# One transfer of score maxima moved to ScalarE's queue, two image transfers merged, and the residual's second LayerNorm one pipeline step later

## The reference, cut to what matters

```
h = edge(x)                      # x: 32 images, 3 x 256 x 256; gray image, two 3x3 Scharr filters, (|gx|+|gy|)/2
h = concat([cls_tok, h])         # 257 tokens of 256 values per image
h = h + attention(layernorm(h))  # 16 heads of 16 values, causal; qkv with bias, output projection with bias
h = h + ffn(layernorm(h))        # gate, up, down with 704 hidden values; weights and activations rounded to 8 bits
```

## Time and profile before

| | |
|---|---|
| median of 3 runs | 1163.3 us (1157.46 to 1168.16) |
| the profiled execution, its own time | 1157.32 us |
| its span, first to last instruction | 1155.6 us |
| mean granted TensorE clock | 0.955 of full speed |
| busy: PE, DVE, ACT, POOL | 989.1, 814.8, 686.6, 538.1 us |
| DMA | 152.93 MB, mean 132 GB/s |

### The profile page before, as it was taken

The page is one execution under the profiler, slowest core; times in us unless marked ns, Lnnn a source line. Parts: engine busy times, 40 slices in busy tenths (PEclk is TensorE's granted clock), DMA queues, the critical chain, the costliest instruction groups (busy, mean ns, idle before and its releaser), DMA issues. The chain is left out here.

```text
span 1155.6 us, 28368 instructions
## 1 busy us (share of the span) xinstructions
PE 989.1 (86%) x9742; PEld 709.7 (61%) x9742; DVE 814.8 (71%) x1969; ACT 686.6 (59%) x1171; POOL 538.1 (47%) x685
## 2 busy tenths in 40 slices
PE   6768989899999999899999998999888888887665
PEld 5446766666667676667676676676676643333454
DVE  4565566766677777766777777666666449998787
ACT  1345555666666566666666666665553237876776
POOL 5335455565555655565556555655443242220000
PEclk7888999999999999999999999999998989998989
DMA  7665555555556555555565555453422005501874
GB/s 200 149 138 145 132 136 143 133 128 134 133 154 151 137 148 148 129 130 138 152 152 135 149 148 130 130 139 100 116 63 63 12 1 200 200 1 50 265 227 151
DMA packets 156017, 152.93 MB, mean 132 GB/s; under 512 B 28175, under 2 KB 152372, under 8 KB 153908
## 3 DMA queue, kind: packets, MB, share of 16 engines
q1 hardware_dynamic: 154440, 152.14, 48.7%
q10 hardware_dynamic: 1516, 0.01, 0.1%
HBM read 67.49 MB, written 28.35 MB: 83 GB/s over the span
## 5 line engine op out<-in xcount | busy, mean ns | idle before, releaser
L580 ACT ACTIVATE prob<-ST 128x772 f32<-128x772 f32 x256 | 209.5, 818 | 152.4 <-PE ST L1022 147.7
L788 DVE TENSOR_REDUCE mneg<-SX 128x2 f32<-128x258 f32 x256 | 107.5, 420 | 224.7 <-PE SX L1008 224.5
L1005 PE MATMUL SX<-kst,qst 96*128 96x257 bf16 (+1 forms) x1024 | 160.4, 250 | 18.3 <-DMA qst<-qpart 7.6
L790 DVE TENSOR_REDUCE mneg<-SX 128x2 f32<-128x514 f32 x256 | 173.9, 679 | 0.0
L1022 PE MATMUL ST<-qst,kst 98*128 98x256 bf16 (+2 forms) x1536 | 138.0, 222 | 16.3 <-DMA qst<-mpart 15.9
L465 POOL TENSOR_SCALAR_AFFINE_SELECT prob<-prob 128x1016 f32<-128x1016 f32 x128 | 142.6, 1114 | 0.0
L1008 PE MATMUL SX<-mask_s,ident_b 128*128 128x256 bf16 x512 | 142.4, 278 | 0.0
L1022 PEld LDWEIGHTS ST<-qst,kst 98*128 98x128 bf16 x1536 | 120.3, 99 | 34.5 <-DMA qst<-mpart 14.7
L1005 PEld LDWEIGHTS SX<-kst,qst 96*128 96x128 bf16 x1024 | 91.9, 99 | 64.3 <-issue 28.4
L1041 PE MATMUL G<-prob,vaug 128*32 128x256 f32 (+2 forms) x3072 | 116.2, 280 | 11.9 <-POOL prob L465 10.6
L1041 PEld LDWEIGHTS G<-prob,vaug 128*32 128x32 f32 x3072 | 82.7, 111 | 44.6 <-POOL prob L465 16.0
(11 more groups left out here) (232 smaller groups left out, 2056.9 us busy)
## 6 DMA issues: line engine op xcount, KB each, us to landing
kst<-kpart SPq DMA_DIRECT2D x192, 128.5 KB, 2.5
xin<-in_x SPq DMA_DIRECT2D x96, 256.0 KB, 4.1
gst<-gray_dram SPq DMA_DIRECT2D x96, 256.0 KB
qst<-qpart SPq DMA_DIRECT2D x192, 128.0 KB, 2.4
h_dram<-hb SPq DMA_DIRECT2D x8, 1280.0 KB, 4.6
gray_dram<-gray SPq DMA_DIRECT2D x64, 128.0 KB, 3.0
result<-oy SPq DMA_DIRECT2D x32, 256.0 KB, 3.6
hb<-h_dram SPq DMA_DIRECT2D x5, 1280.0 KB, 6.6
```

Source lines behind the costliest of these rows:

```text
L580: nc.scalar.activation(prob[:, g % 2, 2 * (u % 2):2 * (u % 2) + 2, 0:QEND], ST[:, :, 0:QEND], ACT.Exp).then_inc(exp_done, 1)
L788: nc.vector.tensor_reduce(mneg[:, 0, u // 4, 0, at], SX[:, :, S0:S0 + P + 1], AX.X, ALU.max, negate=True)
L790: nc.vector.tensor_reduce(mneg[:, 1, u // 4, 0, at], SX[:, :, S1:S1 + T], AX.X, ALU.max, negate=True).then_inc(max_done, 1)
L1005: mm(SX[:, r, at:at + k], qst[par][0:SR, 2 * u + r, P * t:P * t + P], kst[par][0:SR, 2 * u + r, 0:k], start=t == 1, stop=False)
```

## The change

It has three parts. (1) `max_rows(half 1)` is no longer issued by SP at the start of the next step, but by ACT at the end of its step, where ACT now waits for `msplit` (the DVE copy L805 at the start of the next step). (2) The three colour planes of an image are loaded by one DMA in place of three, and the gray image is saved by one in place of two. (3) `resid_stats`, the power on POOL and `x2` with its maxima are done for `bR = n-7` in place of `bO = n-6`, at other places of the step; `LAST` is 7, and `load_down` stands in step 33 in place of the end of step 32.

```diff
-        LAST = 6
+        LAST = 7
...
-        NW0, NW2 = 3, B + LAST - 2
+        NW0, NW2 = 3, B + 4
...
             def load_x(b, par):
-                for c in range(CH):
-                    sp.dma_start(xin[par][:, c, :, :], src[:, c]).then_inc(x_loaded[par], 16)
+                sp.dma_start(xin[par][:, :, :, :].rearrange("p c t w -> p (c t) w"), src).then_inc(x_loaded[par], 16)
...
             def load_down():
-                sp.wait_ge(gray_step, 2 * (B - 1))
+                sp.wait_ge(gray_step, 2 * B)
...
             # SP, step
-                max_rows(bT, odd, 1)
                 if valid(bO):
                     wait(sp, den_moved, bO, 64, 64)
...
                     sp.dma_start(rec[:, :], den[:, :]).then_inc(rec_moved, 16)
+                if isinstance(n, int) and n == B + 1:
+                    load_down()
                 if valid(bW):
...
-                    for t in range(QT):
-                        sp.dma_start(gray_dram[odd][1 + P * t:1 + P * t + P, 1:1 + IMG],
-                                     gray[:, t, :]).then_inc(gray_saved, 16)
+                    sp.dma_start(gray_dram[odd][1:1 + IMG, 1:1 + IMG].rearrange("(t p) w -> p t w", p=P),
+                                 gray[:, :, :]).then_inc(gray_saved, 16)
...
-                if isinstance(n, int) and n == B:
-                    load_down()
...
             # POOL, step
                 select(bT, 1)
+                if valid(bR):
+                    wait(pool, ln2, bR, LN, LN)
+                    wait(pool, x2_step, bR - 1, XS, XS)
+                    nc.gpsimd.tensor_tensor(rstd2[:, rows2(bR)], ve2[:, :], half[:, :], ALU.pow
+                                            ).then_inc(rs2_done, 1)
...
                 select(bS, 0)
-                if valid(bO):
-                    (the same for bO)
                 if valid(n):
                     wait(pool, gray_scaled, n, 3, 3)
...
             # ACT, end of the step
                 exponential(bS, 2)
                 if valid(n):
-                    wait2(act, x_loaded, n, par, 48)
+                    wait2(act, x_loaded, n, par, 16)
                     for c in range(CH):
                         nc.scalar.mul(xin[par][:, c, :, :], xin[par][:, c, :, :], GRAY[c]).then_inc(gray_scaled, 1)
+                if valid(bS):
+                    wait(act, msplit, bS, 2, 2)
+                    act.dma_start(qst[par][SR:SR + 2, 8:16, :], mpart[1][:, :]).then_inc(m_loaded[1], 16)
...
             # DVE, step
                 maxima(bS, 0)
                 (reciprocal of den for bO)
+                resid_stats(bR)
                 maxima(bS, 1)
+                if valid(bR):
+                    (x2, colmax, mean2 for bR)
                 maxima(bS, 2)
...
                 maxima(bS, 6)
-                resid_stats(bO)
                 (vlast and vaug for bP)
                 maxima(bS, 7)
-                if valid(bO):
-                    (x2, colmax, mean2 for bO)
...
-                if isinstance(n, int) and n == B + LAST - 1:
+                if isinstance(n, int) and n == B + 5:
```

More of the change, by code:

```diff
@@ L298, in _ @@
         def _(sp):
-            xv = x.rearrange("b c (t p) w -> b p c t w", p=P)
+            xv = x.rearrange("b c (t p) w -> b p (c t) w", p=P)
             def load_x(b, par):
-                src = xv[b] if isinstance(b, int) else xv[bass.ds(b, 1)].rearrange("o p c t w -> (o p) c t w")
-                for c in range(CH):
-                    sp.dma_start(xin[par][:, c, :, :], src[:, c]).then_inc(x_loaded[par], 16)
+                src = xv[b] if isinstance(b, int) else xv[bass.ds(b, 1)].rearrange("o p k w -> (o p) k w")
+                sp.dma_start(xin[par][:, :, :, :].rearrange("p c t w -> p (c t) w"), src).then_inc(x_loaded[par], 16)
             load_x(0, 0)
@@ L384, in step @@
                 if valid(bW):
-                    wait(sp, gray_saved, bW, 32, 32)
+                    wait(sp, gray_saved, bW, 16, 16)
                     wait(sp, conv_done, bC, 2, 2)
@@ L468, in step @@
             def step(n, par):
-                bC, bP, bS, bT, bO = n - 2, n - 3, n - 4, n - 5, n - 6
+                bC, bP, bS, bT, bR = n - 2, n - 3, n - 4, n - 5, n - 7
                 select(bT, 1)
+                if valid(bR):
[3 more added lines that the diff above has]
+                                            ).then_inc(rs2_done, 1)
                 if valid(bS):
@@ L503, in step @@
                 select(bS, 0)
-                if valid(bO):
[L505 to L508, removed]
                 if valid(n):
                     wait(pool, gray_scaled, n, 3, 3)
-                    wait(pool, gray_saved, n - 1, 32, 32)
+                    wait(pool, gray_saved, n - 1, 16, 16)
                     src = lambda c: xin[par][:, c, :, :]
@@ L854, in step @@
             def step(n, par):
-                bC, bP, bS, bT, bO = n - 2, n - 3, n - 4, n - 5, n - 6
+                bC, bP, bS, bT, bO, bR = n - 2, n - 3, n - 4, n - 5, n - 6, n - 7
                 odd = 1 - par
@@ L862, in step @@
                     nc.vector.reciprocal(den[:, :], den[:, :]).then_inc(rec_done, 1)
+                resid_stats(bR)
                 maxima(bS, 1)
+                if valid(bR):
+                    wait(dve, rs2_done, bR, 1, 1)
+                    for t in range(QT):
+                        nc.vector.tensor_scalar(x2[:, t, :], h2[:, row_of(bR, t), :].rearrange("p o d -> p (o d)"),
+                                                ag2[:, t, 0:1], rstd2[:, row_of(bR, t)],
+                                                ALU.subtract, ALU.mult).then_inc(x2_step, 1)
+                    wait(dve, x2_step, bR, XS, 2)
+                    nc.vector.tensor_reduce(colmax[:, rows2(bR)], x2[:, :, :], AX.X, ALU.max,
+                                            apply_absolute_value=True)
+                    nc.vector.tensor_reduce(mean2[:, rows2(bR)], ag2[:, :, 0:1], AX.X, ALU.max).then_inc(x2_step, 2)
                 maxima(bS, 2)
```

## The result

| | before | after |
|---|---|---|
| median | 1160.0 us (1155.0 to 1168.2, 13 runs) | 1148.5 us (1143.3 to 1154.6, 13 runs) |
| ratio of times, 95% interval | | 0.9895 [0.9867, 0.9922] |
| the profiled execution, its span | 1157.3, 1155.6 us | 1149.6, 1147.9 us |
| mean granted TensorE clock | 0.955 | 0.954 |

The change takes off 11.5 us by the medians and 7.7 us between the two profiled executions. The forecast was 1157, or 6.2 us less than the 1163.3 known then. The interval, 0.8 to 1.3% faster, has the 1% bound inside it.

The account below looks back on a forecast made before the run. The prediction took the steady step as bound by the chain PE -> ACT -> POOL -> PE. Start -0.5, loop -1, step 33 -0.7 and end -4.0 gave -6.2 us, from 1163.3 to 1157; range 1141 to 1167.

Parts of the forecast that it names:

- the removed holes: PE's idle gaps of 0.64 and 0.56 us before outputs(1), claimed to cost nothing in the steady step.
- select wait of some 0.8 us per step: Sign of a right forecast: PE's wait for POOL's select grows to this as other waits shrink.
- the gate: PE's wait at outputs(1) for POOL's select(1), taken to set the steady step's length.
- the 0.06 us margin: At outputs(1): PE arrives when POOL is ready, to 0.06 us, taken as showing the holes upstream cost nothing.
- Loop, -1 (0 to -3): Loop steps where PE comes late to the gate: moved residual statistics save 0 to 3 us, taken as 1.
- Step 33, -0.7: Step 33: load_down no longer holds up half 1, removing a 0.68 us wait of scores_t(4).
- Tail, -4.0 (-2.6 to -4.4): End of the block: earlier last reciprocal and rec issue save 2.6 us, with half 1's earlier arrival 4.0 in all.
- Start, -0.5: Launch start: merged transfers shorten SP's row of first issues, between 0 and -1.0 us.
- (a) The port on the gate: Loop: L852 before select(1) makes POOL wait, 0.36 us in each of 31 steps; +6 us, 1169; chance 0.11.
- (b) The holes count: Loop: the closed holes shorten each of 31 steps, -16 to -23 us; 1135 to 1142; chance 0.14.
- (c) Nothing arrives: Tail's PE work holds spread_rec and the loop gains nothing: 1163 us; chance 0.15.

Follow-up runs that it names:

- e7: The changed kernel plus three idle DVE reductions in front of split: 1146.45 us, ratio 0.9904 to the kernel before.
- e11: The changed kernel plus one small idle power on POOL behind the gray additions: 1178.1 us, ratio 1.0174 to the kernel before.
- e5: The kernel before with POOL's gray additions moved behind select(1) from step 8 on: 1159.2 us, ratio 1.0013.
- e3: The kernel before with part 3 of the change alone: 1150.35 us, ratio 0.9925.
- e10: The kernel before with part 3 for all but the last two images, load_down in step 33, LAST 6: 1155.8 us, ratio 0.9974.
- e2: The kernel before with part 2 of the change alone, the merged image transfers: 1160.5 us, ratio 1.0005.
- e4: The kernel before with only load_down moved one step later, to step 33 behind the rec transfer: 1154.8 us, ratio 0.9980.
- e8: The kernel before with part 3 for the last two images only: 1152.1 us, ratio 0.9933.
- e1: The kernel before with part 1 alone, half 1 of the maxima issued by ACT: 1158.5 us, ratio 1.0012.
- e9: The changed kernel with POOL's gray additions after select(1) and after the rstd2 power: 1162.7 us, ratio 1.0036 to the kernel before.
- e12: e9 with x2 and its reductions moved behind maxima(6), except in the last steps: 1163.6 us, ratio 1.0028 to the kernel before.

## Why the prediction was right, and where it was off

**The mechanism held, the size was low.** The forecast had PE bound by PE -> ACT -> POOL -> PE, and the removed holes worth little. The wait moved to `outputs(1)` (0 to 0.42 us a step), the chain kept its length (7.02 and 7.00), 0.6 us of delay in front costs nothing (e7), and 0.93 or 1.32 us more on the chain cost 0.95 or 1.32 a step (e11). Two qualifications. I expected a select wait of some 0.8 us per step; by the same count it is 14.9/24, about 0.62. And the gate was not the only bound before: opening it alone (e5) gives nothing that the medians show, so PE's own path through the holes was nearly as late, as the 0.06 us margin said, but I read that margin as one-sided.

**Loop, -1 (0 to -3).** Right in kind, undersized. Per step 459.7/18 = 25.54 us in place of 462.4/18 = 25.69, by the means of the groups: -2.7 us in 18 steps. Between the two marks the steps before lie between 25.56 and 25.86, and after between 25.43 and 25.55 but for one of 25.75. That the holes counted in those steps in which PE came late to the gate is my reading; no run shows it by itself. The early steps give no clear answer: up to the first mark the kernels of the table without the deferral need 303.9 to 311.1 us and those with it 303.3 to 311.1, counted by transposes. In this pair the changed kernel is 2.3 us later there, most of it from the copy at 204.50 / 202.45 to that at 257.05 / 260.42: 57.97 us after and 52.55 before, with e3 at 55.78, e10 at 52.33, e2 at 55.07. These overlap, and their cause stays open.

**Step 33, -0.7.** This step of the prediction failed, although it moved the forecast little. I put the long steps down to `load_down` in front of half 1. e4 takes that 0.68 us wait away and the steps stay long (82.86). What was long in them were stretches at 1.2 GHz; with the changed kernel they are gone, and that gives 2.8 us in this pair. The forecast priced TensorE at one clock.

**Tail, -4.0 (-2.6 to -4.4).** Right in mechanism, and in size for what it priced: `rec` is issued 3.82 us earlier, counted from the last transpose. Its -2.6 for the statistics alone is what e8 shows (2.6). The other 1.4 were put down to half 1 on ACT's queue and the earlier copy; part 1 is not needed for it, as e3, without part 1, issues `rec` 19.72 us after the transpose and the changed kernel 20.39. The clock, which was in no term, adds 2.3 in this pair and 1.3 by the means. By medians e8 gives -0.67% [-0.94, -0.39], some 8 us, more than its profile's 4.3, and e10 only -0.26% [-0.51, -0.01], some 3 us, less than the 2.7 + 4.0 of loop and three steps. So how the gain divides between loop and tail is known to about 3 us only.

**Start, -0.5, and part 1 and 2 at nothing.** e1 and e2 show no change to within 0.3%, which could still hide 0.5 us.

**The rivals.** (a) The port on the gate: L852 starts at 417.22, just before the select at 417.29, and neither is delayed. In the whole loop it takes 189 ns on average in place of 456, so the move took it out of the conflict. The price was real, however, at another place: `x2` beside POOL's `vcls` takes 1.01 us in place of 0.74, which no wait of PE's list shows, and in e9 and e12 the conflict took back at least a part of what an open gate could give. The Trainium skill, "SBUF — State Buffer", section "SBUF: two separate sides", says that DVE operations of certain kinds and GpSimd's lock each other out for a whole instruction. The trace agrees: 2.51 us for 0.74 beside the gray additions. In e12 a DVE operation ran from 428.47 to 431.30 beside three of POOL's in a row, `vcls`, key part and select, and ended only 0.28 us after the last; the page speaks of one instruction. (b) The holes count: only as 0.15 us a step, where this rival had 0.5 to 0.7. It would have given 1135 to 1142. (c) Nothing arrives: refuted by e3 and e8.

**The time and luck.** 1148.5 lies between the forecast of 1157 and (b)'s 1142, so the time alone would not have told them apart; e7, e11 and the wait at `outputs(1)` do. The range held it because it took in the nearer parts of the rivals; to a time under 1151.7 I had given a chance of 0.21. Of the 8.6 us between the sum's 1157.1 and the time, 3.3 are the kernel before, whose median came down from 1163.3 (3 runs) to 1160.0 (13 runs), and 5.3 are the change, -6.2 forecast and -11.5 measured. By the means of the profiles the parts of the gain are 2.7 (loop), 4.0 (three steps) and 5.1 us (end), 11.8 in all, where the sum had 1, 0.7 and 4.0. The clock's share in the last two was in no term.

## What to carry to other kernels

An idle gap in front of a gate that opens later is worth little or nothing, and the place to look is the last wait on a chain through several engines; to prove a gate, lengthen its link by a known amount and see whether the step grows by as much. Where PE waits in a drain stage, price the matmuls behind the wait at both clocks, and look at several kernels or executions before you credit a change with the faster one: here a long wait always met 1.2 GHz behind it, a short one often too. Divide a step-by-step comparison at marks that the change itself does not move. When two engines share a port, moving an operation out of one overlap moves its neighbours into another, so add up the durations of all groups that can meet, not only the one moved.

## What was not expected of the hardware

- One DMA issue for 768 KB takes 0.41 us on SP, three for 256 KB each 1.53; the issue's time does not go with the bytes. The merged load lands 5.7 us after its issue in the median, a single plane 4.1, as the DMA lists of the two profiles have it.
- An issue on ACT's queue for the two rows of maxima took 0.62 us, about SP's 0.69, not the 0.32 of the earlier trace rows.
- DVE's `x2`, one 128x256 source and two columns, ended with POOL's operations beside it: two of them take 0.74 us alone, 1.01 beside one of a single partition (1x256), and 2.51 beside the gray additions. The first edge tile of a step (two 128x256 sources) went from 0.85 us after to 2.83 in e12; the second, with POOL idle, took 0.43 after. BATCH_NORM_STATS2 beside the second gray addition (416.04, in the changed kernel) kept its 0.74.
